# One attention and expert layer on one core: the parts' way through DRAM, the first pieces' order, and where in the line sends are issued

## What is computed

```python
B, S, D, H = 2, 1024, 256, 16           # encoder rows: 77; experts E = 8, two of them for each row
def _attn(q_in, k_in, v_in, wq, bq, wk, bk, wv, bv, wo, bo, causal):
    Q = (q_in @ wq + bq).reshape(Bq, Sq, H, HD)
    Kp = (k_in @ wk + bk).reshape(Bq, Sk, H, HD)
    V = (v_in @ wv + bv).reshape(Bq, Sk, H, HD)
    scores = einsum('bqhd,bkhd->bhqk', Q, Kp) / sqrt(HD)   # causal: masked
    o = einsum('bhqk,bkhd->bqhd', softmax(scores), V)
    return o @ wo + bo
x = _layernorm(x + _attn(x, x, x, ..., True), ln1_g, ln1_b)
x = _layernorm(x + _attn(x, encoder_output, encoder_output, ..., False), ln2_g, ln2_b)
x = _layernorm(x + _moe(x, router_w, router_b, w1, b1, w2, b2), ln3_g, ln3_b)
```

## Time and profile before

| | us |
|---|---|
| median of three runs | 770.86 |
| lowest, highest | 767.49, 771.93 |
| profiled execution, its own time | 766.46 |
| its span | 764.7 |
| PE busy | 715.7 (94%) |
| DVE busy | 499.0 (65%) |
| ACT busy | 369.7 (48%) |
| POOL busy | 285.3 (37%) |

### The profile page before, as it was taken

How to read it: one execution, slowest core, us unless ns; L and a number is a source line. 1 busy time by engine, 2 the same in 40 slices (tenths; PEclk the granted TensorE clock), 3 DMA queues, 4 the chain that set the end, 5 groups by cost and what they waited for, 6 DMA issues and landing times. The chain is left out here.

```text
span 764.7 us, 14565 instructions
## 1 busy us (share of the span) xinstructions
PE 715.7 (94%) x4969; PEld 479.3 (63%) x4969; DVE 499.0 (65%) x1376; ACT 369.7 (48%) x749; POOL 285.3 (37%) x558
## 2 busy tenths in 40 slices
PE   6889999999999999999987899996999999999983
PEld 4444434545464454645653586896999999999941
DVE  4579787678766877756785745462656666666436
ACT  3325475665766676677742456332423323332403
POOL 7305521543653463634652343203222322332114
PEclk9999999999999999999995999999899999999997
DMA  8955331343164022315029654667699999999764
GB/s 257 281 142 147 99 111 45 83 127 127 36 175 126 13 60 66 95 54 142 14 72 326 214 167 133 237 221 256 245 334 340 327 339 347 338 337 326 236 190 156
DMA packets 95154, 140.29 MB, mean 183 GB/s; under 512 B 11855, under 2 KB 81077, under 8 KB 92597
## 3 DMA queue, kind: packets, MB, share of 16 engines
q1 hardware_dynamic: 76357, 107.86, 45.0%
q10 hardware_dynamic: 15072, 22.02, 8.6%
q0 software_dynamic: 3648, 9.45, 3.3%
HBM read 110.65 MB, written 28.65 MB: 182 GB/s over the span
## 5 line engine op out<-in xcount | busy, mean ns | idle before, releaser
L1468 DVE TENSOR_REDUCE neg_part_max<-work 128x1 f32<-128x512 f32 (+4 forms) x368 | 213.3, 625 | 66.5 <-PE work L934 36.0
L1242 ACT ACTIVATE arena<-score_pair 128x1024 f32<-128x1024 f32 (+2 forms) x224 | 178.9, 840 | 80.3 <-PE score_pair L960 73.9
L931 PE MATMUL work<-arena 96*128 96x77 bf16 (+4 forms) x640 | 118.0, 277 | 10.4 <-ACT arena L1205 2.7
L983 PE MATMUL out_acc<-arena 128*32 128x512 f32 (+4 forms) x896 | 106.5, 521 | 2.7 <-ACT arena L1242 1.8
L960 PE MATMUL score_pair<-arena 99*128 99x512 bf16 (+2 forms) x448 | 103.5, 335 | 2.5 <-DMA arena<-negmax_scratch 1.5
L854 PE MATMUL score_pair<-arena 128*128 128x256 f32 x432 | 97.6, 379 | 0.0
L931 PEld LDWEIGHTS work<-arena 96*128 96x128 bf16 x640 | 49.0, 98 | 74.2 <-issue 30.2
L1956 POOL TENSOR_SCALAR_AFFINE_SELECT arena<-arena 128x256 f32<-128x256 f32 x128 | 51.5, 410 | 117.8 <-ACT arena L1242 116.6
L1900 POOL DMA_INDIRECT chosen_scratch<-arena,scatter_rows x36 | 35.3, 980 | 145.4 <-DVE arena L1400 143.8
L848 PE MATMUL work<-arena 128*128 128x128 f32 x720 | 88.0, 279 | 0.5 <-issue 0.3
L1175 ACT ACTIVATE arena<-work,expert_b_cols 128x128 f32<-128x128 f32 x180 | 51.2, 370 | 77.0 <-PE work L848 63.8
(11 more groups left out here) (257 smaller groups left out, 961.3 us busy)
## 6 DMA issues: line engine op xcount, KB each, us to landing
arena<-in_L_xattn_e_w SPq DMA_DIRECT2D x54, 1024.0 KB, 6.9
arena<-parts_scratch SPq DMA_DIRECT2D x24, 768.0 KB, 6.1
arena<-in_L_xattn_e_w ACTq DMA_DIRECT2D x18, 1024.0 KB, 6.6
parts_scratch<-arena_more SPq DMA_DIRECT2D x24, 384.0 KB, 2.6
parts_scratch<-arena_more SPq DMA_DIRECT2D x24, 256.0 KB, 2.9
parts_scratch<-arena_more SPq DMA_DIRECT2D x24, 128.0 KB, 3.0
residual<-in_x SPq DMA_DIRECT2D x4, 512.0 KB, 8.4
tokens_scratch<-residual SPq DMA_DIRECT2D x2, 1024.0 KB, 4.8
```

Of the source, the lines that this page charges most:

```text
L931: m = pe.matmul(bank[:, j * it.w:(j + 1) * it.w], qa[st.half(it.g)][0:R_S, h, n0:n0 + P], k, start=True, stop=not it.last)
L983: m = pe.matmul(o_ps[c * VW:(c + 1) * VW, skip:QG], v, pt[buf][0:rows, j, 0:QG - skip], start=first, stop=last)
L1242: act_e.activation(pt[buf][0:rows, :, 0:w], st2[pair][0:rows, :, 0:w], ACT.Exp, scale=float(HD) ** -0.5).then_inc(pair_taken[pair], 1)
L1468: dve.tensor_reduce(pm[:, it.at, it.t, it.h0:it.h0 + it.nh], bank[:, 0:it.nh * it.w].rearrange("p (j k) -> p j k", j=it.nh), AX.X, ALU.max ...
```

## The change

`parts_d` holds three planes instead of six for queries and for keys. `store` becomes one DMA of the three parts; `load` becomes three DMAs for queries and three for keys, reading runs of 3, 2 and 1 planes into 48, 32 and 16 partitions (`RUNS`); keys' parts lie in reverse order in SBUF (`part_of`), so that each run is contiguous. The pairs of parts are the same six in another order. `columns` becomes an item of its own on DVE and is moved, with its PE part, ahead of the first projection, and the first projection ahead of the fifth and sixth transposes. `t_weights` is split in three items, one for each tile. Letters B, A, Z, D and one U stand elsewhere in `ORDER`. In the diff below the two strings are cut to the pieces that differ.

```diff
+RUNS = ((0, 3, 0, 0), (3, 2, 0, 1), (5, 1, 0, 2))
+NPART = 3
+Q_PART = [a + i for _, n, a, _ in RUNS for i in range(n)]
+K_PART = [NPART - 1 - b - i for _, n, _, b in RUNS for i in range(n)]
-    work = [..., Item("first"), Item("t_weights"), Item("tiles"), Item("experts")]
+    work = [..., Item("first"), Item("tiles"), Item("experts")]
+    work += [Item("t_weights", t=j) for j in range(RING1)]
-parts_d = nc.dram_tensor("parts_scratch", [2 * B * (H // HH), 2, NG, NGR, P, QG], bf16, ...)
+parts_d = nc.dram_tensor("parts_scratch", [2 * B * (H // HH), 2, NG, NPART, P, QG], bf16, ...)
# ORDER, start
-x6prbpxvrs2l
+x4bprx2pxvrs2l
# ORDER, sends of weights
-FqBqXwuawax2Oa2xkxIdudpdA3rpt2NADWsrNA2lU2
+Fq2BXwuawax2Oa2xBkxIdudpdA3rpt2NADWBsrNA2lU2
# ORDER, scatters of results (Z) and gathers (A)
-onUhVYyUnonNn3qnqnena3U2YR2wuMahyMq2d
+onUhVYyUnonNZn3qnqnena3U2YR2wuZMahyMq2d
-wudqZUwuUd2PtNtotoZto2eU2Ya4zNUYR2LRLRZUNK
+wudqUwuUd2PZtNtototo2eU2YaZa3zNUYR2LRLRUZNK
-KSZTUNU2YU2EOIAZXZY2ZA2Z2DW
+KSTUZNU2YUZUEOIA3XDY2Z2W
# ACT
                 elif it.kind == "t_weights":
...
-                    for j in range(RING1):
-                        weights1(j)
-                        if j < RING2:
-                            weights2(j)
+                    weights1(it.t)
+                    if it.t < RING2:
+                        weights2(it.t)
# DVE
+                elif it.kind == "columns":
+                    e.wait_ge(w_self_in[1], 16)
+                    dve.tensor_copy(*heads_apart(w_self[1], w_landed[1])).then_inc(self_apart, 1)
+                    e.wait_ge(bias_in, 16 * NCOL // KC)
+                    dve.tensor_copy(b_apart..., b_rows...).then_inc(apart_ok, 1)
+                    e.wait_ge(full[it.bank], it.use)
+                    dve.tensor_copy(b_col[:, :], bank[:, 0:NCOL]).then_inc(taken[it.bank], 1)
+                    e.wait_ge(w_self_in[0], 16)
+                    dve.tensor_copy(*heads_apart(w_self[0], w_landed[0])).then_inc(self_apart, 1)
+
                 elif it.kind == "proj" and st.in_a_hurry:
-                    if it.n == 0:
-                        for i in (1, 0):
-                            e.wait_ge(w_self_in[i], 16)
-                            dve.tensor_copy(*heads_apart(w_self[i], w_landed[i])).then_inc(self_apart, 1)
-                        e.wait_ge(bias_in, 16 * NCOL // KC)
-                        ...
# SP, store
-                    for first, n, part, step in (Q_RUNS, K_RUNS)[it.at]:
-                        ...
-                        sp.dma_start(parts_d[st.n, it.at, it.g, first:first + n, :, 0:it.w].rearrange("g p t -> p g t"),
-                                     src).then_inc(parts_out[ring_of[key]], 16)
+                    sp.dma_start(parts_d[st.n, it.at, it.g, :, :, 0:it.w].rearrange("k p t -> p k t"),
+                                 parts[:, :, it.t:it.t + it.w]).then_inc(parts_out[ring_of[key]], 16)
# SP, load
-                        sp.dma_start(to.rearrange("p h t -> p (h t)"),
-                                     parts_d[st.n, at, it.g].rearrange("g (d h) t -> (g d) (h t)", h=HH)).then_inc(
-                            qk_in[st.half(it.g)], 16)
+                        for first, n, *part0 in RUNS:
+                            sp.dma_start(to[first * HD:(first + n) * HD].rearrange("p h t -> p (h t)"),
+                                         parts_d[st.n, at, it.g, part0[at]:part0[at] + n].rearrange(
+                                             "k (d h) t -> (k d) (h t)", h=HH)).then_inc(qk_in[st.half(it.g)], 16)
```

More of the change, by code:

```diff
@@ L27 @@
 VW = 2 * HD
[L32 to L36, removed]
+RUNS = ((0, 3, 0, 0), (3, 2, 0, 1), (5, 1, 0, 2))
+NPART = 3
+Q_PART = [a + i for _, n, a, _ in RUNS for i in range(n)]
+K_PART = [NPART - 1 - b - i for _, n, _, b in RUNS for i in range(n)]
+assert sorted(zip(Q_PART, K_PART)) == sorted((a, b) for a in range(NPART) for b in range(NPART - a))
 NGR = len(Q_PART)
-NRUN = len(Q_RUNS)
+NRUN = len(RUNS)
 R_S = NGR * HD
@@ L287, in all_work @@
     st = [Stage(n, n >= 4, (n // 2) % 2, n % 2) for n in range(8)]
-    work = [Item("columns"), Item("b1"), Item("b2"), Item("first"), Item("t_weights"), Item("tiles"), Item("experts")]
+    work = [Item("columns"), Item("b1"), Item("b2"), Item("first"), Item("tiles"), Item("experts")]
     for cross in (False, True):
@@ L608, in build @@
             sent_before[key] = sent[ring_of[key]]
-            sent[ring_of[key]] += 16 * NRUN
+            sent[ring_of[key]] += 16
             sent_after[key] = sent[ring_of[key]]
@@ L614, in build @@
             where = it.st.half(it.g)
-            so_far[where] = so_far.get(where, 0) + (16 if it.st.cross else 32)
+            so_far[where] = so_far.get(where, 0) + 16 * NRUN * (1 if it.st.cross else 2)
             landed[it.st.n, it.g] = so_far[where]
@@ L1194, in scalar @@
                     bias = b_col[:, n:n + 1]
-                    to = part_sb[ring_of[key] // NG][:, 0, it.t:it.t + it.w]
+                    to = part_of(it, 0)
                     e.wait_ge(full[it.bank], it.use)
@@ L1208, in scalar @@
                 elif it.kind == "rest" and st.in_a_hurry:
-                    key = st.n, it.at, it.g
-                    z = projected[key]
+                    z = projected[st.n, it.at, it.g]
                     e.wait_ge(taken[z.bank], z.use)
-                    act_e.copy(part_sb[ring_of[key] // NG][:, 1, it.t:it.t + it.w],
-                               f_sb[z.n % 2][:, 0:it.w]).then_inc(second_part, 1)
+                    act_e.copy(part_of(it, 1), f_sb[z.n % 2][:, 0:it.w]).then_inc(second_part, 1)
                 elif it.kind == "v":
@@ L1940, in gpsimd @@
                 if it.kind == "rest" and not st.in_a_hurry:
-                    key = st.n, it.at, it.g
-                    z = projected[key]
-                    f, p = f_sb[z.n % 2][:, 0:it.w], [part_sb[ring_of[key] // NG][:, k, it.t:it.t + it.w] for k in range(3)]
+                    z = projected[st.n, it.at, it.g]
+                    f, p = f_sb[z.n % 2][:, 0:it.w], [part_of(it, k) for k in range(NPART)]
                     e.wait_ge(taken[z.bank], z.use)
@@ L2072, in sync @@
                         e.wait_ge(parts_out[ring_of[key]], sent_after[key])
-                        sp.dma_start(kac[st.slot][0:R_S, :, 0:SE], parts_d[st.n, 1, 0, :, :, 0:SE].rearrange(
-                            "g (d h) t -> (g d) h t", h=HH)).then_inc(kac_in[st.slot], 16)
+                        for first, n, _, part0 in RUNS:
+                            sp.dma_start(kac[st.slot][first * HD:(first + n) * HD, :, 0:SE],
+                                         parts_d[st.n, 1, 0, part0:part0 + n, :, 0:SE].rearrange(
+                                             "k (d h) t -> (k d) h t", h=HH)).then_inc(kac_in[st.slot], 16)
                 elif it.kind == "load":
```

49 lines of the change are left out of this document (21 added, 28 removed).

## The result

| | before | after |
|---|---|---|
| median, us | 770.88 | 782.27 |
| lowest to highest, us | 767.49 to 771.93 | 781.67 to 783.40 |
| profiled execution: time, span, us | 766.46, 764.7 | 781.67, 779.9 |
| PE busy, us (share) | 715.7 (94%) | 722.8 (93%) |
| granted clock, mean | 0.978 | 0.967 |

The change makes the kernel slower: after over before is 1.0153, with an interval of 1.0116 to 1.0190. I had forecast 762.4 us and a range of 755.5 to 769.5; the direction was wrong, and the time lies outside the range. No rival described it either: the slower one had its cause at the last `lay`, the half rate behind which was only a small part of what came (a ratio in this text is given with a 95% interval).

A forecast was written before the change was run, and what follows sets the result against it. PE, busy 94% of the span, was taken as the bound, with time to win only in its waits or low clock. Terms +1.2, -5.0, +2.5 and -7.2 gave -8.5 us: 758.0 profiled, 762.4 at the median, range 755.5 to 769.5.

The forecast's parts named there:

- the slower one: Rival: idle ahead of the last `lay` brings a long half clock; +6.7 us in all, 777.6 us, chance 0.06.
- start: Columns ahead of the first projection wait for bias rows; first maxima move by +1.2 us, bounds -0.5 and +2.5.
- parts' way, outside the start: Stores in one DMA, loads in three, through DRAM: taken as 0 us, between -2.3 and +2.
- sends of weights: Weight sends moved on ACT's queue around cross-attention's exponentials: -5 us, bounds -3 and -6.5.
- scatter ahead of the last gather: On POOL, the second `Z` holds the gather that PE's `lay` needs: +2.5 us, bounds +1 and +6.
- end of the line: Scatters of tiles 4 to 6 go ahead of a gather; PE's wait shrinks, clock stays up: -7.2 us, bounds -3.5 and -8.
- the page's estimate: Loads of parts: were the three pieces serial, fixed cost per DMA would add about 4 us a load.
- The -3.7: Sends: PE's second weigh in cross-attention, no longer cut in two, ends at 409.7 instead of 413.4 us.
- the -1.3: Sends: gain from a higher clock with denser PE work, to the end of the 401.5 to 420.6 us slice; bounds 0 and -3.
- "0 to +2": Sends: cost in us of the last 1 MB flying beside the parts' load of 768 KB, against a store shorter by 1.
- The clock's fall behind it: Scatter on POOL: upper bound of +6 us if the clock falls again around the last `lay`.
- The base: Profiled execution of 766.46 us lay 4.4 below the median 770.86; that difference was carried over from 758.0 to 762.4 us.

The follow-up runs named there:

- e12: The kernel before with only the start changed (columns ahead of the first projection, that ahead of the fifth and sixth transposes): 773.50 us, 1.0061.
- e2: The kernel before with only the new stores and loads of parts (three planes, one store DMA, loads in runs of 3, 2 and 1): 780.41 us, 1.0107.
- e11: The kernel before with only the sends of the first expert weights split and moved on ACT's queue: 770.96 us, 1.0012.
- e1: The kernel after with the stores and loads of parts of the kernel before; new line, columns and sends kept: 773.20 us, 1.0035.
- e8: e1 with the second scatter put back behind the last gather of maxima: 768.06 us, 0.9990 of the kernel before.
- e10: The kernel before with only the end of the line changed (scatters of tiles 4, 5 and 6 ahead of the gathers behind the list): 764.19 us, 0.9927.
- e7: The kernel after with its three planes laid out so that each load is three even pieces of 32 partitions: 773.99 us, 1.0052 of the kernel before.
- e9: e8 with the start of the kernel before put back: 764.99 us, 0.9925 of the kernel before.
- e3: The kernel before with 24 loads of queries and keys each cut in three DMAs of 48, 32 and 16 partitions: 782.75 us, 1.0143.

## Why the prediction was wrong

By the ratios of single changes, times 771 us (the scatter's as the difference of two):

| step | my sum, us | measured, us (interval) | run |
|---|---|---|---|
| start | +1.2 | +4.7 (+2.8 to +6.6) | e12 |
| parts' way, outside the start | 0 | +8.2 (+4.6 to +11.8), with the start's share | e2 |
| sends of weights | -5.0 | +0.9 (-1.4 to +3.2) | e11 |
| scatter ahead of the last gather | +2.5 | +3.5 (-0.5 to +7.4) | e1, e8 |
| end of the line | -7.2 | -5.6 (-8.0 to -3.3) | e10 |
| sum | -8.5 | +11.7 | after: +11.8 |

The five add up to what the whole change does. Their errors together are about 7 us, so a cause smaller than that, or an interplay of the five, could still hide in the sum; one as large as the whole loss is not missing.

**Parts' way: the step that failed.** I took the load in three pieces at 0, between -2.3 and +2, from "a store in three pieces is what they show". That row answered the question whether pieces in flight overlap, and they do. It could not answer the one that counted, since a store in three pieces still touches all 128 partitions of SBUF in each; no row of before had a DMA with a boundary at partition 48 or 80. The serial fixed costs that I had set beside it as the page's estimate (4 us more a load; the section has its 2.0 us for DMAs that GpSimd issues, and these are issued by SP) are not what happened, as the even cut shows; it was a third thing. With one even cut in the place of the uneven one the whole change comes down from 782.27 to 773.99 us. The bound of +2 was too narrow for an operation that the trace had never shown, 28 times over.

**Start.** The mechanism and each time to the queries' third part held within 0.7 us (the last is at 21.19, forecast for 21.7). Wrong was the price: I let 1.5 us come back through the shorter way, and it did not (first maxima at 32.30 us with one store and even loads, e7, beside 32.28 with three stores, e1); and one trace's start was taken as the typical one, 1.1 us late against the mean of its kind. With the bad cut the first maxima came at 35.05.

**Sends.** The -3.7 is in the trace of `e11_sends_alone`, between 406 and 412 us; of the -1.3 nothing is, as it falls back by 0.7 us between 418 and 424. The term that failed is the last one, "0 to +2" for 1 MB beside the parts' load, taken as if paid by the shorter store. The wait there was 2.5 us longer with the sends alone and 5.9 in e9, in both with a fall of the clock, which the term had not at all; in e1 it was 0.2 us longer, so the size changes from one execution to the next. The row for it was at hand: rows 7 have a wait of 1.4 us at just this load, so there was no slack, and the send of tile 3's weights (431.85) follows tile 0's progress and moves forward with it. The Trainium skill, DMA: Bandwidth & Descriptors, "Issuing engines are not separate DMA queues", says it (sends from ACT and loads from SP share the same 16 engines), and these runs agree: a store of 3.1 us took 12.0 between them. I had drawn on that rule for the end of the line, where it mattered least.

**Scatter on POOL.** Right in the wait: 2.3 us for 2.5. The clock's fall behind it, a bound of mine, came on top: 3.1 us more in the trace of the line alone, 1.8 in the kernel after.

**End of the line.** Right in place, releaser and clock; 6.3 us by the medians for 7.2. In the kernel after, 5.4 us came back between 528 and 545 us.

**The base.** The profile of before ran 4.4 us below its median. It has no fall of the clock between 387 and 398 us; the trace of after and those of all experiments have one, and fall back there by 1.7 to 3.3 us against it, whatever their edit. Most also fall back behind 700 us, by 1.4 to 3.0 us. Carrying the difference to the median was right; reading a start and slack from one trace as typical was not.

## What to carry to other kernels

When an edit changes the shape of a DMA, a row of the same size is no price for it: look whether the partitions that it touches begin and end where those of the row do, and time the cut itself. Of the cuts tried here only three even pieces of 32 partitions cost nothing; 64+32 cost 0.8% though both boundaries lie at multiples of 32. When a transfer is moved in time, list what else is in flight at the new place, the sends that follow from progress too, and ask whether a wait for one of them is already there; such a wait has no slack. Where PE has work all the time, expect a delay at the start to be paid in full, and moving an instruction that has to wait ahead of one that is ready to cost the whole wait and a fall of the clock behind it, as both did here.

## What the runs showed of the hardware

- A load of 0.79 MB into 96 partitions took 3.17 us of packet time on each DMA engine uncut, 3.28 in three pieces of 32, but 4.07 in pieces of 48, 32 and 16 and 3.72 in 64, 16 and 16: up to 28% more for the same bytes.
- Three DMAs in place of one, back to back on one queue, in 24 loads, cost nothing that can be measured (1.0006, 0.9970 to 1.0042): no fixed cost added up in the kernel's time.
- Behind a wait of PE of 2.16 us the granted clock was 0.50 (1.2 GHz) in one trace (e3), and around one of 2.34 us 0.59 (e1). The fall cost 3.2 and 3.1 us on top of the wait in these two, and 1.8 behind a wait of 2.34 us in the kernel after.
- A store of 384 KB with a median of 3.1 us took 12.0 us between two transfers of 1 MB.
